# Two slots in one instruction: VectorE's product and scan, GpSimd's product, with the driven states in SBUF

## The reference, cut to what matters

```python
delta = softplus(einsum('blr,dr->bld', dt, dt_w) + dt_b)
dA  = exp(delta[..., None] * A)                       # decay,   (B, L, d_inner, 16)
dBu = delta[..., None] * Bm[:, :, None, :] * xi[..., None]   # driven
def step(h, inp):
    dA_t, dBu_t, C_t = inp
    h = dA_t * h + dBu_t                              # the recurrence over L = 1024
    return h, einsum('bds,bs->bd', h, C_t)            # product with C, sum over 16 states
y = ys + xi * Dp
```

## Time and profile before

| | us |
|---|---|
| median of 3 runs | 4236.63 (4227.06 to 4249.97) |
| the profiled execution, its own time | 4219.27 |
| its span, first to last instruction | 4217.4 |
| VectorE busy in the span | 3493.2 (83%) |
| TensorE busy | 3708.7 (88%) |
| ScalarE busy | 2772.9 (66%) |
| GpSimd busy | 2345.8 (56%) |

### The profile page before, as it was taken

How to read it: one execution, slowest core, us unless ns; L and a number is a source line. 1 busy time by engine, 2 the same in 40 slices (tenths; PEclk the granted TensorE clock), 3 DMA queues, 4 the chain that set the end, 5 groups by cost and what they waited for, 6 DMA issues and landing times.

```text
span 4217.4 us, 41720 instructions
## 1 busy us (share of the span) xinstructions
PE 3708.7 (88%) x14008; PEld 1348.4 (32%) x14008; DVE 3493.2 (83%) x3101; ACT 2772.9 (66%) x3212; POOL 2345.8 (56%) x1092
## 2 busy tenths in 40 slices
PE   6889988899879998899988999889988899878887
PEld 2332234222342223422244222432234322342223
DVE  2379987799778997699976999679987799778997
ACT  2567757777576775677666775767657767576764
POOL 0138762578426874177732787238762477426873
PEclk9999999999999999999999999999999999998878
DMA  1158861698518884288724887268961698507881
GB/s 40 35 144 214 214 166 47 169 220 205 134 51 207 206 220 100 72 215 219 206 63 119 214 209 171 75 146 212 217 167 47 165 220 201 141 18 196 199 204 46
DMA packets 186045, 644.72 MB, mean 153 GB/s; under 512 B 25660, under 2 KB 26600, under 8 KB 182280
## 3 DMA queue, kind: packets, MB, share of 16 engines
q1 hardware_dynamic: 168808, 596.95, 57.9%
q10 hardware_dynamic: 17024, 45.10, 3.5%
HBM read 525.40 MB, written 78.82 MB: 143 GB/s over the span
## 4 chain that ended last, share of the span: by engine, by line
DVE 35%; issue 25%; PE 18%; ACT 13%; DMA 4%; POOL 4%; SPq 0%; DVEq 0%; ACTq 0%; POOLq 0%
DVE ps L1571 15%; DVE arena L1576 13%; PE ps L673 4%; DMA arena<-dl 3%; PE ps L613 3%; PE ps L664 2%; ACT arena L1036 2%; ACT arena L1018 2%; POOL arena L1689 2%; POOL arena L1680 2%; ACT arena L1240 2%; PE ps L692 2%; DVE arena L1424 1%; ACT L1152 1%; ACT arena L1029 1%
## 5 line engine op out<-in xcount | busy, mean ns | idle before, releaser
L1680 POOL TENSOR_TENSOR arena<-arena 128x1024 f32<-128x1024 f32 x760 | 1785.9, 2359 | 704.3 <-DVE arena L1576 704.3
L1576 DVE TENSOR_TENSOR_SCAN arena<-arena,ps 128x1024 f32<-128x1024 f32 x768 | 1756.4, 2287 | 74.6 <-issue 31.6
L1240 ACT ACTIVATE arena<-arena,a_all 128x1024 f32<-128x1024 f32 x768 | 869.8, 1146 | 692.1 <-DMA arena<-dl 541.4
L834 PE MATMUL ps<-arena,spread 32*128 32x512 f32 x1536 | 876.4, 652 | 142.7 <-DVE arena L1576 140.9
L1571 DVE TENSOR_TENSOR ps<-ps,arena 128x1024 f32<-128x1024 f32 x768 | 928.3, 1209 | 57.5 <-PE ps L836 57.2
L836 PE MATMUL ps<-arena,spread 32*128 32x512 f32 x1536 | 869.1, 653 | 0.0
L857 PE MATMUL ps<-arena,gather 128*32 128x512 f32 x3072 | 519.4, 629 | 12.5 <-DVE arena L1587 12.4
L928 PE MATMUL ps<-x 96*96 96x512 f32 x1008 | 499.1, 613 | 26.5 <-ACT arena L1171 26.5
L834 PEld LDWEIGHTS ps<-arena,spread 32*128 32x128 f32 x1536 | 230.1, 186 | 785.9 <-DVE arena L1576 482.8
L1638 POOL TENSOR_TENSOR x<-x,arena 96x512 f32<-96x512 f32 x64 | 113.9, 1780 | 377.1 <-DVE arena L1415 377.1
L993 ACT ACT_TABLE_LOAD x226 | 290.0, 1283 | 24.7 <-DMA wo<-in_wo 20.7
(11 more groups left out here) (160 smaller groups left out, 4907.8 us busy)
## 6 DMA issues: line engine op xcount, KB each, us to landing
arena<-dl SPq DMA_DIRECT2D x880, 512.0 KB, 6.9
dl<-arena ACTq DMA_DIRECT2D x64, 384.0 KB, 5.9
x<-pn SPq DMA_DIRECT2D x56, 247.5 KB, 10.5
arena<-in_x SPq DMA_DIRECT2D x9, 1536.0 KB, 13.2
arena<-xq SPq DMA_DIRECT2D x64, 192.0 KB, 6.2
arena<-arena ACTq DMA_DIRECT2D x64, 192.0 KB, 7.5
out<-x SPq DMA_DIRECT2D x64, 192.0 KB, 2.1
arena<-xq SPq DMA_DIRECT2D x64, 191.8 KB, 5.5
```

The lines of the kernel that those rows point to most:

```text
L834: pe.matmul(ps[:, bank, :], spread[rows[0], r, :], u[rows[0], i, 0:512], start=True, stop=True)
L1240: act.activation(da[:, m % DAS, :], dbc[:, m % DBC, :], ACT.Exp, scale=a_all[:, v // 2, m:m + 1]).then_inc(da_ready, 1)
L1576: dve.tensor_tensor_scan(hs[:, m % HSS, :], da[:, m % DAS, :], driven, 0.0, ALU.mult, ALU.add).then_inc(h_ready, 1)
L1680: pool.tensor_tensor(product, product, cmat[:, v % 2, :], ALU.mult).then_inc(pr_ready, 1)
```

## The change

Pairs of slots are handled together. DVE's product with B, for two slots in one instruction of 128x2048, reads the four PSUM banks and writes into two adjacent slots of `hs` in SBUF. One scan of 128x2048 then runs through both, in place in `hs`, with the decays of two adjacent buffers; the decay of each slot's first position is set to zero, so the second half starts a fresh recurrence (ACT writes `da[:, :, 1:L]` only, and POOL clears column 0 once a pair). POOL's product with C is 128x2048 as well. The first two slots of a pair and the last two keep single instructions on DVE. `DAS` becomes 4, `HSS` 8; TensorE lays the broadcasts of the next two slots at the even step, and waits for the product (`bu_ready`) instead of the scan. The small tables `st` and `nrm` move into the arena, which grows to 32270 columns.

```diff
-DAS = 3
-HSS = 6
+DAS = 4
+HSS = 8
-ARENA = 30300
+ARENA = 32270
-        st = sb("st", [128, 8, ST])
-        nrm = sb("nrm", [128, 6, ST + 2])
+        st = cut(128, 8 * ST).rearrange("p (k s) -> p k s", k=8)
+        nrm = cut(128, 6 * (ST + 2)).rearrange("p (k s) -> p k s", k=6)
+        def one_slot(v, m):
+            return (v == 0 and m < 2) or (v == UNITS - 1 and m >= G - 2)
@@ tensor
                     if v or m >= 2:
-                        pe.wait_ge(h_ready, n - 1)
+                        pe.wait_ge(bu_ready, n - m % 2)
+                def first():
+                    broadcast_u(0, 0)
+                    broadcast_u(0, 1)
+                    states_first()
-                    w, k = after(v, m, 1)
-                    if w < UNITS:
+                    w, k = after(v, m, 2)
+                    if m % 2 == 0 and w < UNITS:
                         broadcast_u(w, k)
-                    if v == 0 and m == 0:
-                        states_first()
+                        broadcast_u(w, k + 1)
@@ scalar
-                    act.activation(da[:, m % DAS, :], dbc[:, m % DBC, :], ACT.Exp,
+                    act.activation(da[:, m % DAS, 1:L], dbc[:, m % DBC, 1:L], ACT.Exp,
@@ vector
+                def scan(v, m, count):
+                    V = p * UNITS + v
+                    n = V * G + m
+                    h, d, b = (v * G + m) % HSS, m % DAS, 2 + 2 * (m % 2)
+                    driven = ps[:, b:b + 2 * count, :].rearrange("p (s b) n -> p s (b n)", s=count)
+                    state = hs[:, h:h + count, :]
+                    dve.wait_ge(ubc_ready, n + count)
+                    if v or m + count > HSS:
+                        dve.wait_ge(y_acc, V * GPB + (m + count - 1 - HSS) // TRIO + 1)
+                    dve.tensor_tensor(state, driven,
+                                      bmat[:, v % 2, :].rearrange("p (o n) -> p o n", o=1)
+                                      .broadcast_to([128, count, L]), ALU.mult).then_inc(bu_ready, count)
+                    dve.wait_ge(bu_ready, n + count)
+                    if v == 0 and m == 0:
+                        dve.wait_ge(da_zero, p + 1)
+                    dve.wait_ge(da_ready, n + count)
+                    line = state.rearrange("p s n -> p (s n)")
+                    dve.tensor_tensor_scan(line, da[:, d:d + count, :].rearrange("p s n -> p (s n)"), line, 0.0,
+                                           ALU.mult, ALU.add).then_inc(h_ready, count)
-                    driven = two(2 + 2 * (m % 2))
-                    dve.wait_ge(ubc_ready, n + 1)
-                    dve.tensor_tensor(driven, driven, bmat[:, v % 2, :], ALU.mult).then_inc(bu_ready, 1)
-                    dve.wait_ge(bu_ready, n + 1)
-                    dve.wait_ge(da_ready, n + 1)
-                    if v or m >= HSS:
-                        dve.wait_ge(y_acc, V * GPB + (m - HSS) // TRIO + 1)
-                    dve.tensor_tensor_scan(hs[:, m % HSS, :], da[:, m % DAS, :], driven, 0.0,
-                                           ALU.mult, ALU.add).then_inc(h_ready, 1)
+                    if one_slot(v, m) or m % 2 == 0:
+                        scan(v, m, 1 if one_slot(v, m) else 2)
@@ gpsimd
+                pool.memset(da[:, :, 0:1], 0.0).then_inc(da_zero, 1)
-                    if v < UNITS - 1 or m < G - 1:
-                        pool.wait_ge(h_ready, n + 1)
-                        product = hs[:, m % HSS, :]
-                        pool.tensor_tensor(product, product, cmat[:, v % 2, :],
-                                           ALU.mult).then_inc(pr_ready, 1)
+                    if v == UNITS - 1 and m == G - 2:
+                        products(v, m, 1)
+                    elif m % 2 and (v < UNITS - 1 or m < G - 1):
+                        products(v, m - 1, 2)
+                def products(v, m, count):
+                    pool.wait_ge(h_ready, p * UNITS * G + v * G + m + count)
+                    h = (v * G + m) % HSS
+                    pool.tensor_tensor(hs[:, h:h + count, :], hs[:, h:h + count, :],
+                                       cmat[:, v % 2, :].rearrange("p (o n) -> p o n", o=1)
+                                       .broadcast_to([128, count, L]), ALU.mult).then_inc(pr_ready, count)
```

More of the change, by code:

```diff
@@ L266, in program @@
         xs_zero = sem("xs_zero")
+        da_zero = sem("da_zero")
         xi_ps = sem("xi_ps")
@@ L857, in states @@
                             mm = pe.matmul(ps[b * BLK:(b + 1) * BLK, c, :], gather[:, r, :],
-                                           hs[:, (r * TRIO + b) % HSS, c * 512:(c + 1) * 512],
+                                           hs[:, (v * G + r * TRIO + b) % HSS, c * 512:(c + 1) * 512],
                                            start=False, stop=(r == GPB - 1), skip_group_check=True)
@@ L963, in final @@
                     project(QUADS - 1, 1, 7)
-                scan_stage(prep, lambda: broadcast_u(0, 0), step, conv, final)
+                scan_stage(prep, first, step, conv, final)
                 pe.wait_ge(mo_copied, (p + 1) * 2 * QUADS)
@@ L1244, in first @@
                     decay(0, 0)
+                    decay(0, 1)
                     for c in range(2):
                         first_states(c, 6 + c, first_c_ps, cmat, first_c)
-                    for m in range(1, DAS - 1):
+                    for m in range(2, DAS - 1):
                         decay(0, m)
@@ L1584, in final @@
                     n = V * G + G - 1
-                    q, i, slot = QUADS - 1, (UNITS - 1) % 2, (G - 1) % HSS
+                    q, i, slot = QUADS - 1, (UNITS - 1) % 2, (UNITS * G - 1) % HSS
                     dve.wait_ge(h_ready, n + 1)
@@ L1669, in step @@
                 def step(v, m):
-                    V = p * UNITS + v
-                    n = V * G + m
                     if m == 0 and v:
```

## The result

The changed kernel takes 5234.2 us (median of three executions), 1.236 times the kernel before (95% interval 1.231 to 1.241); 5258 was forecast. The profiled execution's span is 5232.4 us against 4217.4: +1015 us where +1022 was forecast.

The account below looks back on a forecast made before the run. VectorE's chain of product and scan, 3.44 us a step, was taken to bound the scan stage. Exclusion with GpSimd added 1022 us to the profiled 4219.3, plus 17 for the median: 5258 us, range 5110 to 5430.

Parts of the forecast that it names:

- The bound and the exclusion: Scan stage: VectorE bounds; its two-SBUF-input scan and GpSimd's SBUF-reading work wait out each other's whole instruction, +1022 us; chance 0.82.
- the first rival: Scan beside GpSimd's product: ports shared by turns, not whole instructions; +316 us, near 4550 us; chance 0.06.
- doubled period: From one doubled scan's end to the next, with exclusion: 8.90 us against 6.89 for two steps before.
- GpSimd's other work: GpSimd's L1667, L1689 and L1697 no longer hide beside VectorE's scans: 40.6 us a pair.
- TensorE "well under 80%": Sign in the profile after: TensorE's busy share of the stage of some 465 us, with VectorE near 100%.
- Edits taken at nothing: Broadcasts, decays in twos, product's wait for free slots, GpSimd's column clearing and moved tables: all covered, no cost.
- The fourth buffer gives two steps of lead: ScalarE's decays, now coming in twos after a scan, cost nothing thanks to this lead and 86 us idle a stage.
- The second rival: Scan at L1576 doesn't touch the path shared with GpSimd: -96 us alone, near 4140 us; chance 0.08.
- the 96 us: VectorE's saving from doubled product and scan: 0.26 us per doubled pair of steps, over 368 in the run.

Follow-up runs that it names:

- The operand alone: Kernel before, with only the product with B written to SBUF and the scan reading both operands there, single slots everywhere: 5319.9 us, 1.255 times before.
- the threshold in GpSimd's columns: Changed kernel with GpSimd's product with C cut to the first 64 columns of each slot: 4360.3 us; cut to 512 columns: 4406.9 us.
- the clearings: Changed kernel with GpSimd's product with C replaced by two memsets of the same slots, which only write SBUF: 4365.5 us, 1.032 times before.

## Why the prediction was right, and where it wasn't

- **The bound and the exclusion**: right. The step that decided was to read what VectorE's L1587 did to GpSimd's L1697 and to carry it over to a scan that no row showed. The operand alone (5320 us), the threshold in GpSimd's columns and the clearings each support it, and the scan with its driven values in PSUM shows the other side. Turn by turn, the first rival, is out: GpSimd's product keeps its 4.52 us while the scan waits. The direction that the earlier trace rows showed only for a cast, GpSimd first, holds for a scan.
- **The sizes**: product with B 2.26 forecast, 2.259 measured; doubled scan 4.42, 4.42; GpSimd's product 4.54, 4.52; doubled period 8.90, 8.95; GpSimd's other work 40.6 a pair, about 36 (465.0 - 5.7 - 46 x 8.95 - 11.4); a pair's stage 467, 464.9 to 465.3 in the first seven pairs; the last 459.4, 456.4. The 40.6 count L1697 six times a pair; it runs eight times (56 in seven pairs), seven of them before the last scan, so the sum should have had 1.3 us more there and was still too high. The eight stages sum to 1004 of the 1015 us where 1022 were forecast; the other 11 lie outside them, and what they are is open. That the total came within 7 us is in part luck: 18 too many in the stages, 11 outside them not foreseen.
- **TensorE "well under 80%"** was wrong: 368 of 465 us is 79%, since its clock fell to 0.82 on average and the same 1126 records took 368 us in place of 318.
- **"Edits taken at nothing"** was right for this kernel and wrong as a rule. "The fourth buffer gives two steps of lead" overlooked that three load buffers can't fill that lead: alone it costs some 120 us. GpSimd's doubled product, priced only by its length, alone costs 380, since TensorE's queue waits for it. In the changed kernel the longer period covers both: its doubled products wait for nothing and its doubled scans 34 us in all.
- **The second rival's price**, 4140 us without contention, was wrong. With GpSimd's product all but taken away it is 4360, with half the loads 4255; less the 47 and 54 us of contention left in them, that would be some 4310 and 4200 (an estimate). The term that failed is the one that took the 96 us as all there is: it counted what VectorE's instructions save and not what two slots at once ask of loads, ScalarE and TensorE. The forecast's side and size didn't hang on it, but a forecast for a kernel whose GpSimd reads nothing meanwhile would have missed.

## What to carry to other kernels

Before an operand is moved from PSUM to SBUF, look at what GpSimd does at that time: here a VectorE product or scan with two SBUF inputs and a GpSimd instruction that reads SBUF took turns by whole instructions, so what overlapped before added up (4.42 us of scan became 6.69). Any row where two such instructions overlap tells it, even a short one at the end of a stage. And an instruction over two units asks all its suppliers for two at once: count the buffers and the queue places behind it before booking the saved fixed parts.

## What the runs showed of the hardware that was not expected

- Where two GpSimd instructions follow each other directly, a waiting scan is sometimes let in between and sometimes not. The scan recorded at 339.10 stood through the rest of L1728 and through all of the product that began at 340.17, and took 9.87 us; so it went in all 49 such places of the changed kernel's trace. But between the product at 328.02 and the gate at 332.51 the scan went first, and the gate waited, in all 56 such places. With GpSimd's product cut to 512 columns the scan went first behind the addition too: the scan at 322.73 took 5.38 us and the product that began at 323.79 took 6.46 in place of 2.36. What decides is not shown.
- Clearing SBUF from GpSimd (1.80 us for 128x2048) runs beside a scan with two SBUF operands without delay to it (the scan keeps its 4.42 us).
